# Key stacking moved ahead of the tree gathers in a perceiver kernel on one NeuronCore

## The chip, the cores and the metric

The kernel runs on one core of one Trainium2 chip. The metric is device time in microseconds (us) of one execution; lower is better. Engines in the text: PE (TensorE), DVE (VectorE), ACT (ScalarE), POOL (GpSimd), SP (SyncE, which issues transfers), and the 16 DMA engines of the core. The three runs shown gave 647.74, 648.18 and 651.8 us.

## The reference, cut to what matters

A residual stream `x` of 128 tokens by 128 features goes through twelve blocks; `ctx` has 2048 rows. Three blocks matter here: a linear attention (L1 attn), a block of four hard-routed trees (L1 ffn), and the cross attention behind it (L2 xattn), whose keys and values depend on `ctx` alone.

```python
def _fff(x, nw, nb, w1, b1, w2, b2, act):
    node = jnp.zeros(x.shape[:2], dtype=jnp.int32)
    for _ in range(DEPTH):                     # DEPTH = 8
        logit = jnp.einsum('bsd,bsd->bs', x, nw[node]) + nb[node]
        node = 2 * node + 1 + (logit > 0).astype(jnp.int32)
    leaf = node - NN
    h = act(jnp.einsum('bsd,bsdl->bsl', x, w1[leaf]) + b1[leaf])
    return jnp.einsum('bsl,bsld->bsd', h, w2[leaf]) + b2[leaf]
...
q = _fff(xn, q_nw, ...); k = _fff(xn, k_nw, ...); v = _fff(xn, v_nw, ...)
att = jax.nn.softmax(jnp.einsum('bqd,bkd->bqk', q, k) / jnp.sqrt(D), axis=-1)
...                                            # the fourth tree, f, runs on the sum of this attention and xn
x = x + _L1_attn_ref(...)
x = x + _L1_ffn_ref(...)
x = x + _L2_xattn_ref(_layernorm(x), ctx_1024, W_q, W_k, W_v, W_o, b_o)
```

Each of the 128 tokens picks its own leaf of 256, so each tree needs 128 leaves of 16 x 128 weights and 16 biases (first layer, 1.06 MB) and 16 x 128 weights and 128 biases (second layer, 1.11 MB).

## The kernel before, in words

The blocks run one after another; each is a Python function that appends its instructions to the five engines' streams (`l1a` the linear attention, `l1f` the trees, `cross` the cross attention). Each engine runs its own stream in order. Semaphores order the engines: `T`, `V`, `A`, `G` count steps of PE, DVE, ACT and POOL, and each transfer has its own (`loaded`). There is no scheduler; the order is written out by hand.

In `l1f`, PE turns the normalised tokens and computes the logits of all nodes of the trees q, k and v. DVE then walks the trees (`walk_vector`, first q, then k and v together) and writes one leaf number per token. POOL gathers the leaves by these numbers (`tree_gather`: two indirect transfers per tree, first and second layer; their places are in `leaves`). For each tree, DVE takes 16 products with running sums for the 16 units (`tree_vector`), DVE and ACT scale the second layer's weights by the units, eight rows of them each (`tree_scalar`), and PE sums 17 blocks of 128 x 128, each of them two passes (`tree_tensor`). Ahead of these stand `WARM` = 30 small bf16 products whose results nobody reads. The fourth tree, f, depends on the attention over q, k and v, so its walk and its gather come last.

Into this are woven the keys and values of the next cross attention. PE projects the keys from `ctxT` (four products of 512 columns, `keys_tensor`), ACT rounds them to a high half in `probsT` (`keys_scalar`), DVE subtracts to get the low half in `keysT` (`keys_vector`). The values (16 products, `values_tensor`) use the same banks, so they wait for the low halves; ACT copies them out (`values_scalar`). The high and low halves are then stacked from SBUF to SBUF by 13 transfers on SP's queue (`stack_keys`): twelve of 32 partitions by 8 KB, and one of 9 x 64 pieces of 512 bytes. Their destination holds the third leaf (tree k) until PE has summed it, so SP waits for that:

```python
leaves = {n: region[:, o:o + LEAF] for n, o in (("q", 0), ("v", LEAF), ("k", 2 * REG), ("f", 0))}
...
sp.wait_ge(T.sem, T.at(("o", "k")))
stack_keys(sp, "l2x", wide_high)
sp.wait_ge(T.sem, T.at(("o", "f")))
load("w_l2f", region[:, 0:REG], dram["w_l2f"])
```

Of the kernel before, what the change touches and what calls it, by code (L numbers as in the profile page):

```python
# [106 lines left out]
def build(nc, dram, out, scratch):  # L107
    ctx = ExitStack()
    with ctx:
# [74 lines left out]

        leaves = {n: region[:, o:o + LEAF] for n, o in (("q", 0), ("v", LEAF), ("k", 2 * REG), ("f", 0))}
        w_b_at = 2 * REG - width(W_B) - width(W_C)
# [102 lines left out]
        def _(sp):  # L289
# [19 lines left out]
            load("w_c", region[:, w_b_at + width(W_B):2 * REG], dram["w_c"])  # L309
            sp.wait_ge(T.sem, T.at(("o", "k")))  # L310
            stack_keys(sp, "l2x", wide_high)
# [34 lines left out]
        def turn_plan(tag):  # L346
            T.plan(tag + ".turned")
            V.plan(tag + ".T")
# [1007 lines left out]
        def l1a():  # L1356
# [8 lines left out]
            turn_plan("l1a.o")  # L1365
            T.plan("l1a.y")
            V.plan("l1a.x")

            @on("pe")
            def _(pe):  # L1370
# [13 lines left out]
                pe.wait_ge(V.sem, V.at("l1a.o.T"))  # L1384
                mm(ps[:, 0, 0:P], tG[:, :], at["w_l1a_p"]).then_inc(T.sem, T.now("l1a.y"))

            @on("dve")
            def _(dve):
# [14 lines left out]
                turn_vector(dve, "l1a.o", tG, 7)  # L1403
                end_vector(dve, tag, ps[:, 0, 0:P], xb[:, :], "l1a.y")

            @on("pool")
# [19 lines left out]
        def tree_gather(pool, n):  # L1426
            i = TREES.index(n)
            for layer, dst in ((1, leaves[n][:, 0:LEAF1]), (2, leaves[n][:, LEAF1:LEAF])):
                nc.gpsimd.indirect_dma_start(dst, None, dram[f"tree{layer}_{n}"], bass.IndirectOffsetOnAxis(
                    leaf_no[:, i:i + 1], 0)).then_inc(loads[f"leaf{layer}_{n}"], 16)  # L1430
# [5 lines left out]
        def second(n, c):  # L1436

            return leaves[n][:, LEAF1 + 4 * c * P:LEAF1 + 4 * (c + 1) * P]

        def tree_tensor(pe, n, turned):  # L1440
            o = ps[:, 4 + TREES.index(n), 0:P]

            loaded(pe, "leaf1_" + n)
            for _ in range(WARM):
                mm(ps[:, 0, 0:P], identb[:, :], identb[:, :])
            for c in range(4):
                made = A if c >= 2 else V
                pe.wait_ge(made.sem, made.at(("p", n, c)))
                for j in range(5 if c == 3 else 4):

                    w = second(n, c)[:, j * P:(j + 1) * P] if j < 4 else leaves[n][:, LEAF - P:LEAF]
                    if turned:
                        m = mm(o, w, ident, c == j == 0, j == 4)
                    else:
                        m = mm(o, ident, w, c == j == 0, j == 4)
            m.then_inc(T.sem, T.now(("o", n)))

        def tree_vector(dve, n, x, func=False):
            loaded(dve, "leaf1_" + n)
            h = units(n)  # L1460
            w1 = leaves[n]
            for j in range(LW):
# [64 lines left out]
        def l1f():  # L1527
# [6 lines left out]
            V.plan("l1f.xh")  # L1534
            turn_plan("l1f.xh")
            T.plan("l1f.nodes")
            T.plan(*(("l2x", "kp", b) for b in range(NB)))
            A.plan(*(("l2x", "k", b) for b in range(NB)))
            values_plan("l2x")
            V.plan("l1f.pathq", "l1f.paths", *(("l2x", "low", b) for b in range(NB)))  # L1540
            for n in "qkv":
# [9 lines left out]
            turn_plan("l1f.y")  # L1551
            T.plan("l1f.nodef")
            V.plan("l1f.pathf")
            tree_plan("f", True)
            V.plan("l1f.x")
# [3 lines left out]
            def _(pe):  # L1559
# [7 lines left out]

                loaded(pe, "w_b")
                for b in range(NB):
                    keys_tensor(pe, "l2x", at["w_b.l2x_k"], b, 3 + b)  # L1570
                values_tensor(pe, "l2x", at["w_b.l2x_v"], (7, 3, 4, 5), (None, 0, 1, 2))
                pe.wait_ge(A.sem, A.at(("l2x", "v", 3)))
                tree_tensor(pe, "q", True)
# [8 lines left out]
                pe.wait_ge(V.sem, V.at("l1f.y.T"))  # L1582
                mm(logits(0), xnT[:, :], nodew[:, 3 * NODES:4 * NODES]).then_inc(T.sem, T.now("l1f.nodef"))
                tree_tensor(pe, "f", False)

            @on("dve")
            def _(dve):
# [12 lines left out]
                                        ALU.mult).then_inc(V.sem, V.now("l1f.xh"))  # L1600
                turn_vector(dve, "l1f.xh", xnT)
                loaded(dve, "node")
                dve.wait_ge(T.sem, T.at("l1f.nodes"))
                walk_vector(dve, 0, 1, "l1f.pathq")
                dve.wait_ge(V.sem, V.at("l1f.pathq"))
                walk_vector(dve, 1, 2, "l1f.paths", 1)
                for b in range(NB):
                    keys_vector(dve, "l2x", None, b, 3 + b, wide_high)
                for n in "qkv":
# [23 lines left out]
            def _(act):  # L1633
                for b in range(NB):
                    keys_scalar(act, "l2x", None, b, 3 + b, wide_high)
                values_scalar(act, "l2x", (7, 3, 4, 5))
                for n in "qkv":
                    tree_scalar(act, n)
                act.wait_ge(V.sem, V.at("l1f.m"))
                nc.scalar.activation(tF[:, :], ps[:, 0, 0:P], ACT.Exp, bias=s[:, 1:2], scale=float(1.0 / np.sqrt(P)),  # L1640
                                     accum_out=s[:, 2:3]).then_inc(A.sem, A.now("l1f.p"))
                tree_scalar(act, "f", ACT.Gelu)

            @on("pool")
            def _(pool):
# [11 lines left out]
                pool.wait_ge(T.sem, T.at(("o", "q")))  # L1657
                tree_gather(pool, "f")


# [877 lines left out]
```

## Time and profile before

| what | us |
|---|---|
| runs | 647.74, 648.18, 651.8 (median 648.18) |
| the profiled execution's own time | 649.05 |
| its span in the trace | 647.2 |
| PE busy | 481.8 (74%) |
| DVE busy | 359.8 (56%) |
| ACT busy | 223.2 (34%) |
| POOL busy | 64.6 (10%) |
| DMA queue q1 (SP's transfers) | 33.71 MB, 15.8% of 16 engines' span |
| DMA queue q0 (POOL's gathers) | 8.68 MB, 3.8% |
| mean granted PE clock | 0.839 of full speed |

The busy time says which engine works most, but in a program of dependent blocks the time is set by the chain of waits: the list of instructions, in order of time, each of which released the next. Where one engine is on the chain alone, only that engine's work counts. PE's granted clock has two levels, 0.50 (1.2 GHz) and 1.00 (2.4 GHz). A row of the timeline gives start, duration, engine, source line, operation, what is written from what, and how often; a bracket at its end gives the idle time before it and what ended it.

### The profile page before, as it was taken

To read this page: it belongs to the slowest core of one execution; us is meant where nothing else is said; L and a number is where in the kernel's file an instruction comes from. 1 tells how busy PE (TensorE), PEld (TensorE's weight loads), DVE (VectorE), ACT (ScalarE), POOL (GpSimd) and SP (SyncE) were. 2 spreads that over 40 slices of the span, in tenths; PEclk is the share of its full clock that TensorE was granted. 3 is DMA by queue.
4 is the path that set the end of the run, shared out by engine and by line. 5 is a ranking of instruction groups with operands and counts; after the bars stand their busy time and mean duration, and the time that the engine had idled before them with its cause. 6 is when DMAs were issued, how large, how long until landed. Compare 5 with 4: busy or idle time off the path is not lost.

```text
span 647.2 us, 7837 instructions
## 1 busy us (share of the span) xinstructions
PE 481.8 (74%) x3019; PEld 351.1 (54%) x3019; DVE 359.8 (56%) x795; ACT 223.2 (34%) x439; POOL 64.6 (10%) x105
## 2 busy tenths in 40 slices
PE   3677638999656816799977565778999999866596
PEld 1545524443336805354434344657888888755496
DVE  7356448773349524777526555336666666634433
ACT  0212420778103301155632123316555555501021
POOL 5201002000013010200005104120000000000000
PEclk9787965999757956589988886968999999977679
DMA  7508200000418693600020000000000000045000
GB/s 299 251 3 177 85 1 0 1 1 2 194 53 333 169 180 135 260 1 1 2 90 8 0 1 0 2 1 1 1 1 1 1 1 2 1 162 228 0 1 6
DMA packets 8000, 42.89 MB, mean 66 GB/s; under 512 B 1050, under 2 KB 4122, under 8 KB 4762
## 3 DMA queue, kind: packets, MB, share of 16 engines
q1 hardware_dynamic: 6811, 33.71, 15.8%
q0 software_dynamic: 1152, 8.68, 3.8%
q8 instruction: 24, 0.39, 0.2%
q14 instruction: 13, 0.11, 0.1%
HBM read 35.69 MB, written 0.08 MB: 55 GB/s over the span
## 4 chain that ended last, share of the span: by engine, by line
PE 58%; DVE 28%; ACT 7%; issue 4%; DMA 2%; POOL 2%; POOLq 0%; DVEq 0%; ACTq 0%
PE banks L257 54%; PE banks L260 4%; DVE small L2044 3%; ACT probs L2119 3%; DVE peaks L1282 3%; DVE weights_lo L2054 2%; DMA region<-in_tree_f,leaf_no 2%; DVE xn L338 1%; POOL mv L344 1%; DVE sbq L1511 1%; ACT weights_hi L2132 1%; DVE tB L1786 1%; DVE xnT L357 1%; DVE tA L792 1%; DVE st L334 1%
## 5 line engine op out<-in xcount | busy, mean ns | idle before, releaser
L1282 DVE TENSOR_REDUCE peaks<-banks 128x1 f32<-128x1024 f32 x64 | 76.8, 1221 | 17.2 <-PE banks L257 17.0
L260 PE MATMUL banks<-p_first,probs 128*128 128x128 f32 x320 | 48.6, 288 | 16.6 <-DVE weights_lo L2054 4.4
L2044 DVE TENSOR_REDUCE small<-banks 128x1 f32<-128x1024 f32 x32 | 38.9, 1217 | 29.3 <-PE banks L257 29.3
L2132 ACT CAST weights_hi<-banks 128x512 fp32r<-128x512 f32 x64 | 35.9, 588 | 54.0 <-PE banks L260 54.0
L260 PEld LDWEIGHTS banks<-p_first,probs 128*128 128x128 f32 x320 | 38.3, 147 | 29.3 <-ACT probs L584 4.9
L1341 ACT ACTIVATE probs<-banks,seen 128x512 f32<-128x512 f32 x64 | 40.3, 685 | 27.2 <-PE banks L257 27.2
L2054 DVE TENSOR_TENSOR weights_lo<-banks,weights_hi 128x512 fp32r<-128x512 f32 x64 | 41.6, 682 | 13.0 <-ACT weights_hi L2132 13.0
L1341 ACT ACTIVATE probs<-banks 128x512 f32<-128x512 f32 x64 | 34.8, 595 | 32.9 <-PE banks L257 32.6
L344 POOL TENSOR_TENSOR mv<-mv,half 128x1 f32<-128x1 f32 x15 | 8.3, 553 | 344.8 <-DVE mv L336 344.8
L257 PE MATMUL banks<-probs,values 128*32 128x256 f32 x512 | 41.7, 395 | 0.4 <-DVE keysT L1303 0.4
L2119 ACT ACTIVATE probs<-banks,nmax 128x1024 f32<-128x1024 f32 x32 | 35.4, 1112 | 11.0 <-DVE nmax L2048 10.9
L257 PE MATMUL banks<-weights_hi,rows_hi 128*128 128x256 f32 x128 | 38.3, 299 | 0.0
L257 PE MATMUL banks<-xnT,region 128*128 128x128 f32 (+1 forms) x226 | 36.2, 322 | 1.9 <-DVE xnT L357 1.9
L257 PE MATMUL banks<-weights_lo,rows_hi 128*128 128x256 f32 x128 | 36.9, 288 | 0.0
L257 PE MATMUL banks<-weights_hi,rows_lo 128*128 128x256 f32 x128 | 36.7, 287 | 0.0
L257 PE MATMUL banks<-ctx_hi,query_r 128*128 128x512 f32 x64 | 28.7, 449 | 9.0 <-ACT probs L2119 6.5
L257 PEld LDWEIGHTS banks<-xnT,region 128*128 128x128 f32 (+1 forms) x226 | 33.4, 232 | 3.1 <-DVE xnT L357 3.1
L257 PE MATMUL banks<-keys_l1x,query_r 105*128 105x512 f32 x64 | 26.1, 503 | 4.3 <-DVE query_r L1164 3.2
L257 PE MATMUL banks<-keys_l2x,query_r 105*128 105x512 f32 x64 | 26.3, 507 | 3.3 <-DVE query_r L1164 2.2
L260 PE MATMUL banks<-p_first,xn 128*128 128x128 f32 x10 | 4.2, 418 | 32.6 <-DVE xn L338 32.6
L257 PE MATMUL banks<-region,probs 128*128 128x128 f32 x168 | 23.7, 286 | 4.1 <-ACT probs L670 2.1
L257 PE MATMUL banks<-ctx_hi,query_lo 128*128 128x512 f32 x64 | 26.7, 417 | 0.0
(422 smaller groups left out, 922.4 us busy)
## 6 DMA issues: line engine op xcount, KB each, us to landing
region<-in_w_l2f SPq DMA_DIRECT2D x1, 4096.0 KB, 13.0
region<-in_w_l3f SPq DMA_DIRECT2D x1, 4096.0 KB, 12.1
region<-in_w_b SPq DMA_DIRECT2D x1, 3076.0 KB, 10.3
values<-in_ctx SPq DMA_DIRECT2D x2, 1024.0 KB, 7.7
region<-in_w_l0f SPq DMA_DIRECT2D x1, 2048.0 KB, 20.4
keys_l1x<-shared SPq DMA_DIRECT2D x8, 256.0 KB, 3.9
keys_l2x<-probsT SPq DMA_DIRECT2D x8, 256.0 KB
region<-in_w_l3d SPq DMA_DIRECT2D x1, 2048.0 KB, 17.1
```

Of the source, the lines that this page charges most:

```text
L257: return nc.tensor.matmul(o, lhsT, rhs, start=start, stop=stop)
L260: return nc.tensor.transpose(o, i, ident[0:n, 0:n])
L334: vl(dve, nc.vector.bn_stats(st[:, :], src))
L338: nc.vector.tensor_scalar(xn[:, :], src, mv[:, 0:1], mv[:, 3:4], ALU.subtract, ALU.mult).then_inc(V.sem, V.now(tag + ".xn"))
L344: nc.gpsimd.tensor_tensor(mv[:, 3:4], mv[:, 2:3], half[:, 0:1], ALU.pow).then_inc(G.sem, G.now(tag + ".rstd"))
L357: nc.vector.tensor_copy(dst[0:n, :], ps[0:n, bank, 0:P]).then_inc(V.sem, V.now(tag + ".T"))
L1282: nc.vector.tensor_reduce(peaks[:, h // 4 % 2, i:i + 1], ps[:, 2 * a:2 * a + 2, :], AX.XY, ALU.max, negate=True).then_inc(VM.sem, VM.now(( ...
L1341: nc.scalar.activation(probs[:, u % 8 // 4, u % 4 * BANK:(u % 4 + 1) * BANK], ps[:, 4 + u % 3, :], ACT.Exp, scale=seen[:, 0:1] if masked e ...
L2044: return nc.vector.tensor_reduce(small[:, half:half + 1], ps[:, 2 * half:2 * half + 2, :], AX.XY, ALU.max)
L2054: nc.vector.tensor_tensor(sides(g, c, weights_lo), ps[:, 4 + c % 2, :].rearrange("p (a b) -> p a b", a=4), sides(g, c, weights_hi).bitcast ...
L2119: nc.scalar.activation(probs[:, g % 2, o:o + 2 * BANK], ps[:, 2 * half:2 * half + 2, :].rearrange("p a b -> p (a b)"), ACT.Exp, bias=nmax[ ...
L2132: nc.scalar.copy(sides(g, c, weights_hi), ps[:, 4 + c % 2, :].rearrange("p (a b) -> p a b", a=4)).then_inc(A.sem, A.now((tag, "e", g, c)))
```

## The change

The key projection of the next stage, its ACT halves and its place in the plans move from `l1f` to the end of `l1a`; DVE's low halves move ahead of the first walk. The value projection and its ACT copies move behind the logits of the fourth tree. The third leaf (k) no longer lies where the keys are stacked: its first layer goes to `probs`, its second to `values_t`. So SP's wait for that tree is gone. POOL writes the ones beside the values again, which the leaf has overwritten. The 30 idle products stay for q, become 44 for f, and go for k and v.

```diff
-        leaves = {n: region[:, o:o + LEAF] for n, o in (("q", 0), ("v", LEAF), ("k", 2 * REG), ("f", 0))}
+        spare = probs[:, :, :].rearrange("p a b -> p (a b)")
+        leaves = {n: (region[:, o:o + LEAF1], region[:, o + LEAF1:o + LEAF]) for n, o in (("q", 0), ("v", LEAF), ("f", 0))}
+        leaves["k"] = (spare[:, 0:LEAF1], values_t[:, 0:LEAF - LEAF1])
...
-            sp.wait_ge(T.sem, T.at(("o", "k")))
             stack_keys(sp, "l2x", wide_high)
...
                 mm(ps[:, 0, 0:P], tG[:, :], at["w_l1a_p"]).then_inc(T.sem, T.now("l1a.y"))
+                loaded(pe, "w_b")
+                for b in range(NB):
+                    keys_tensor(pe, "l2x", at["w_b.l2x_k"], b, 3 + b)
...
+            @on("act")
+            def _(act):
+                for b in range(NB):
+                    keys_scalar(act, "l2x", None, b, 3 + b, wide_high)
...
-            for _ in range(WARM):
+            for _ in range({"q": WARM, "f": 44}.get(n, 0)):
                 mm(ps[:, 0, 0:P], identb[:, :], identb[:, :])
...
-                loaded(pe, "w_b")
-                for b in range(NB):
-                    keys_tensor(pe, "l2x", at["w_b.l2x_k"], b, 3 + b)
-                values_tensor(pe, "l2x", at["w_b.l2x_v"], (7, 3, 4, 5), (None, 0, 1, 2))
-                pe.wait_ge(A.sem, A.at(("l2x", "v", 3)))
                 tree_tensor(pe, "q", True)
...
                 mm(logits(0), xnT[:, :], nodew[:, 3 * NODES:4 * NODES]).then_inc(T.sem, T.now("l1f.nodef"))
+                values_tensor(pe, "l2x", at["w_b.l2x_v"], (2, 3, 4, 5), (None,) * 4)
                 tree_tensor(pe, "f", False)
...
                 turn_vector(dve, "l1f.xh", xnT)
+                for b in range(NB):
+                    keys_vector(dve, "l2x", None, b, 3 + b, wide_high)
                 loaded(dve, "node")
...
                 walk_vector(dve, 1, 2, "l1f.paths", 1)
-                for b in range(NB):
-                    keys_vector(dve, "l2x", None, b, 3 + b, wide_high)
...
-                for b in range(NB):
-                    keys_scalar(act, "l2x", None, b, 3 + b, wide_high)
-                values_scalar(act, "l2x", (7, 3, 4, 5))
                 for n in "qkv":
                     tree_scalar(act, n)
...
+                values_scalar(act, "l2x", (2, 3, 4, 5))
                 tree_scalar(act, "f", ACT.Gelu)
...
                 tree_gather(pool, "f")
+                pool.wait_ge(T.sem, T.at(("o", "k")))
+                nc.gpsimd.memset(values_t[:, 0:KT_N * VW].rearrange("p (u w) -> p u w", w=PW)[:, :, 16:18],
+                                 1.0).then_inc(G.sem, G.now("l2x.ones"))
```

On PE, from the end of the linear attention (`p_w_a,tG` is its output projection) to the first product of the next cross attention, the kernel before has these rows; `ctxT,region` are keys, `region,ctxT` values, `identb` the idle products, and `shared,xnT` node logits:

```order
156 L257 MATMUL banks<-p_w_a,tG 128x128
157 L260 MATMUL banks<-p_first,tA 128x128
158 L257 MATMUL banks<-shared,xnT 128x255 x3
159 L257 MATMUL banks<-ctxT,region 128x512 x4
160 L257 MATMUL banks<-region,ctxT 128x128 x16
161 L257 MATMUL banks<-identb 128x128 x30
162 L257 MATMUL banks<-p_first,region 128x128 x17
163 L257 MATMUL banks<-identb 128x128 x30
...
171 L257 MATMUL banks<-shared,xnT 128x255
172 L257 MATMUL banks<-identb 128x128 x30
173 L257 MATMUL banks<-region,p_first 128x128 x17
```

The changed kernel has there:

```order
156 L259 MATMUL banks<-p_w_a,tG 128x128
157 L259 MATMUL banks<-ctxT,region 128x512 x4
158 L262 MATMUL banks<-p_first,tA 128x128
159 L259 MATMUL banks<-shared,xnT 128x255 x3
160 L259 MATMUL banks<-identb 128x128 x30
161 L259 MATMUL banks<-p_first,region 128x128 x17
162 L259 MATMUL banks<-p_first,values 128x128 x17
163 L259 MATMUL banks<-region,p_first 128x128 x17
...
168 L259 MATMUL banks<-shared,xnT 128x255
169 L259 MATMUL banks<-region,ctxT 128x128 x16
170 L259 MATMUL banks<-identb 128x128 x44
171 L259 MATMUL banks<-region,p_first 128x128 x17
```

The keys have moved ahead of the tokens' transpose, the values behind the fourth tree's logits, and the idle products of k and v are gone.

On SP, ahead of the stack of keys, the kernel before has:

```order
27 L283 DMA region<-in_w_b 128x6152 [waits vector_steps]
28 L283 DMA region<-in_w_c 128x1592
29 L283 DMA keys_l2x<-probsT 32x2048 [waits vector_steps,tensor_steps]
30 L283 DMA keys_l2x<-probsT 32x2048
31 L283 DMA keys_l2x<-keysT 32x2048
```

The changed kernel has:

```order
27 L285 DMA region<-in_w_b 128x6152 [waits vector_steps]
28 L285 DMA region<-in_w_c 128x1592
29 L285 DMA keys_l2x<-probsT 32x2048 [waits vector_steps]
30 L285 DMA keys_l2x<-probsT 32x2048
31 L285 DMA keys_l2x<-keysT 32x2048
```

The order is the same, but the stack now waits only for DVE's last low half, no longer for PE's third tree.

## Rows read from the trace of the kernel before

**Rows 1.** Chain of waits in the tree stage: start us, us, what.
```profile
180.99 0.81 PE banks L257 x2
...
186.07 0.36 DVE tA L1599
...
206.38 16.76 PE banks L257 x192
223.16 0.29 DVE tC L1612
...
233.81 10.86 DMA region<-in_tree_f,leaf_no
```

**Rows 2.** Timeline of PE: start us, us, engine, line, operation, passes [idle before].
```profile
187.39 2.92 PE L257 MATMUL banks<-shared,xnT 128*128 128x255 f32 x6 [0.38 <-DVE xnT L357]
190.10 4.80 PE L257 MATMUL banks<-ctxT,region 128*128 128x512 f32 x8
...
200.20 5.49 PE L257 MATMUL banks<-region,ctxT 128*128 128x128 f32 x24 [4.41 <-DVE keysT L1097]
...
206.38 1.85 PE L257 MATMUL banks<-identb 128*128 128x128 bf16 x30 [0.69 <-ACT values L1120]
...
219.11 4.01 PE L257 MATMUL banks<-region,p_first 128*128 128x128 f32 x34
...
244.71 3.38 PE L257 MATMUL banks<-identb 128*128 128x128 bf16 x30 [14.77 <-DMA region<-in_tree_f,leaf_no]
...
249.41 6.21 PE L257 MATMUL banks<-region,p_first 128*128 128x128 f32 x34 [1.32 <-DVE region L1477]
```

**Rows 3.** Timeline of DVE: walk q, low halves, start of trees q and v, products of v.
```profile
190.42 0.42 DVE L1500 TENSOR_TENSOR probs<-banks,shared 128x255 f32<-128x255 f32 x1 [3.08 <-PE banks L257]
...
199.47 2.48 DVE L1097 TENSOR_TENSOR keysT<-banks,probsT 128x512 f32<-128x512 f32 x4
...
201.86 0.28 DVE L1464 CUSTOM_DVE_ANT_0 region<-tA,region 128x128 f32<-128x128 f32 x1
...
212.34 0.29 DVE L1464 CUSTOM_DVE_ANT_0 region<-tA,region 128x128 f32<-128x128 f32 x1
...
216.27 1.29 DVE L1477 TENSOR_TENSOR region<-region,small 128x512 f32<-128x512 f32 x2
```

**Rows 4.** Windows: stretch, us, busy of each engine, granted PE clock, DMA share, GB/s.
```profile
192.00:194.00 2.00, 2.00 (x6) 0.84 (x5) 1.78 (x8) 1.17 (x2) 0.00 (x0) 0.87 0.00 0
...
196.00:198.00 2.00, 0.00 (x0) 0.00 (x0) 1.83 (x11) 0.42 (x1) 0.67 (x1) 1.00 0.84 190
198.00:200.00 2.00, 0.00 (x0) 0.00 (x0) 1.93 (x8) 0.00 (x0) 0.17 (x1) 0.84 1.00 404
...
197.00:213.00 16.00, 12.11 (x108) 11.81 (x109) 15.62 (x94) 6.12 (x18) 3.77 (x4) 0.79 0.97 394
219.00:233.00 14.00, 7.44 (x47) 5.56 (x44) 5.29 (x22) 1.74 (x3) 0.00 (x0) 0.77 0.97 203
235.00:241.00 6.00, 0.00 (x0) 0.00 (x0) 0.00 (x0) 0.00 (x0) 0.94 (x1) 0.50 0.92 114
```

**Rows 5.** Timeline of the issuing queues: SP's w_b, POOL's first v gather, SP's stack.
```profile
169.18 0.33 SPq L283 DMA_DIRECT2D region<-in_w_b  x1
...
202.31 0.94 POOL L1429 DMA_INDIRECT region<-in_tree_v,leaf_no  x1 [0.30 <-issue]
...
217.63 1.15 SPq L283 DMA_DIRECT2D keys_l2x<-probsT  x2
```

**Rows 6.** DMA issues: transfer, queue, how many, KB, median us from issue to landing.
```profile
region<-in_w_b SPq DMA_DIRECT2D x1, 3076.0 KB, 10.3
...
region<-in_tree_q,leaf_no POOLq DMA_INDIRECT x2, 6.4
...
region<-in_tree_v,leaf_no POOLq DMA_INDIRECT x2, 10.7
```

More of the change, by code:

```diff
@@ L1366, in l1a @@
             T.plan("l1a.y")
+            T.plan(*(("l2x", "kp", b) for b in range(NB)))
+            A.plan(*(("l2x", "k", b) for b in range(NB)))
             V.plan("l1a.x")
@@ L1427, in tree_gather @@
             i = TREES.index(n)
-            for layer, dst in ((1, leaves[n][:, 0:LEAF1]), (2, leaves[n][:, LEAF1:LEAF])):
+            for layer, dst in zip((1, 2), leaves[n]):
                 nc.gpsimd.indirect_dma_start(dst, None, dram[f"tree{layer}_{n}"], bass.IndirectOffsetOnAxis(
@@ L1436, in second @@
         def second(n, c):
-            return leaves[n][:, LEAF1 + 4 * c * P:LEAF1 + 4 * (c + 1) * P]
+            return leaves[n][1][:, 4 * c * P:4 * (c + 1) * P]
         def tree_tensor(pe, n, turned):
@@ L1449, in tree_tensor @@
                 for j in range(5 if c == 3 else 4):
-                    w = second(n, c)[:, j * P:(j + 1) * P] if j < 4 else leaves[n][:, LEAF - P:LEAF]
+                    w = second(n, c)[:, j * P:(j + 1) * P] if j < 4 else leaves[n][1][:, LW * P:]
                     if turned:
@@ L1460, in tree_vector @@
             h = units(n)
-            w1 = leaves[n]
+            w1 = leaves[n][0]
             for j in range(LW):
@@ L1535, in l1f @@
             turn_plan("l1f.xh")
+            V.plan(*(("l2x", "low", b) for b in range(NB)))
             T.plan("l1f.nodes")
[L1537 to L1540, printed above, removed]
+            V.plan("l1f.pathq", "l1f.paths")
             for n in "qkv":
@@ L1552, in l1f @@
             T.plan("l1f.nodef")
+            values_plan("l2x")
             V.plan("l1f.pathf")
+            G.plan("l2x.ones")
             tree_plan("f", True)
```

## The prediction

> **What bounds the kernel now.** I read the chain of waits first, since this is one core and one long dependent program: in the tree stage it names what each microsecond goes to. The stretch that the change touches runs from the end of the linear attention (180.99 us) to the first statistics of the next cross attention (about 255.6). The reader is to see three things in it [rows 1]. PE alone carries 206.38 to 223.16: three blocks of idle matmuls to keep the clock up and three sets of 17 transposes. Then follows a serial piece to 233.81 that the change leaves alone. Then 10.86 us are a pure wait for the gather of the fourth leaf. The timeline of PE says why the first block starts as late as 206.38: values of the next stage (24 passes, 5.49 us) stand ahead of it, and wait themselves for DVE's low halves of the keys, which end behind the walks [rows 2, 3]. It also shows the fourth tree's transposes at 6.21 us against 4.01 us for those of the third [rows 2].
>
> The DMA windows come next. While the six gathers of q, k and v run, all 16 engines are busy (share 0.97) at 394 GB/s; while the keys are stacked, they are just as busy (0.97) at 203 GB/s; and while the last, finely cut piece of the stack runs beside the fourth gather, 114 GB/s move in all [rows 4]. Before the change these two crowds are kept apart: gathers from about 197 to 213, stack from 217.63 [rows 4, 5]. DVE starts the third tree at 212.34, and the two v leaves take 10.7 us from issue at 202.31 (and 1.25 later) [rows 3, 5, 6]: that averages 213.65, and at 394 GB/s one leaf half of 1.09 MB takes 2.7, so the first half lands at about 212.3. DVE is therefore already fed by the DMA queue just in time.
>
> **The change, part by part.** All times are those of the profiled execution, span 647.2 us; its own time is 649.05, the median of the runs 648.18, so I add the difference to the median.
>
> *Key projection into the linear attention.* The weights pack w_b was issued at 169.18 and took 10.3, so it is there at 179.5, before PE finishes the linear attention at 181.80 [rows 1, 5, 6]. The eight passes took 4.80 us while the clock rose half way; at 1.2 GHz throughout, scaled from the node logits (2.92 us for six passes of 255 columns), they would take 7.8 [rows 2]. I take 5.9, because before, the clock rose on the way as well (mean 0.87 in the window of 192, after unbroken PE work from 187.39) [rows 2, 4]: 187.7 instead of 186.43 for the transpose that follows. ACT's copies lie beside it. The transpose and DVE's copy then end at 188.4, and four low halves (2.48 us, row of 199.47) come before the walk: DVE starts it at 190.9 instead of 190.42, +0.45. The node logits are hidden under the low halves. The same 2.48 us are gone behind the walks, but that frees DVE only to wait for leaf q.
>
> *The stack moves past the gathers.* SP no longer waits for the third leaf's place, so it issues 13 transfers at 190.9 rather than at 217.63. Twelve of them move 3.15 MB, 15.5 us at 203 GB/s [rows 4]. Bytes flow about 1.2 us after the issue, at 192.1; the gathers' bytes, 0.45 later than before, at 197.45. So 5.35 us of the stack are over and 10.1 us remain, beside 16.5 us of gathers. No row has two streams of long rows at once, so I bound it. If the engines only take turns, the gathers lose all 10.1 us; if the stack's half rate leaves 394 - 203 = 191 GB/s usable, they lose 5.2. The last piece runs about 6 us in which a gather gets 114 - 49 = 65 GB/s (0.29 MB are its own), a loss of 5.0. With the 0.45 the first half of v lands at 227.9 or at 222.95 instead of 212.3; between ends that no row decides I take the middle, 225.4.
>
> The Trainium skill ("DMA: Bandwidth & Descriptors", section "Queues, rings and completion order") says each engine goes round robin over its queues packet by packet; by that the gathers get no precedence, and the sum is the turn-taking one. The same skill ("SBUF — State Buffer", section "Door 1: The DMA port swizzle") says 32 partitions reach only half of the SBUF ports, which would explain 203 beside 394 and speaks for the other bound. Neither is used in the sum.
>
> *Trees.* From the start of a tree DVE needs 216.27 - 212.34 = 3.93 us to its units and 0.65 to the first product, PE then 4.0 for 17 transposes [rows 2, 3]. The dropped idle matmuls of k and v would give back 2 x 1.85 us [rows 2], were PE still the bound; it no longer is. With v at 225.4, k comes some 6 us earlier, PE starts k's transposes cold at about 224 and needs 6.2 (as the fourth tree's), ends at 230.2, and v's then 234.2. Before it was 223.12 [rows 2]: **+11.1 us** (+8.4 and +13.4 at the ends).
>
> *Fourth leaf.* Its gather finds an empty queue. The q leaf did: 6.4 us from issue to landing [rows 6]; now 10.86 [rows 1]. **-4.5 us.**
>
> *Values and 44 idle matmuls before the fourth tree.* Sixteen products (32 passes, at 5.49/24 = 0.23 us each at most 7.3 us) run during the gather wait, which is 6.4 us behind the walk's 3.5: hidden by 2.6 us. Then 44 idle matmuls at 3.38/30 each take 4.96 us, DVE needs 4.7 for the first product, so they delay PE by 0.3, but the transposes then run at 4.01 instead of 6.21 us: **-1.9 us**. PE stood still from 196 on and the clock fell in the window of 198 (mean 0.84) [rows 4]; after the values PE stands still as long, so the 44 must do the warming alone; if they don't, the term is +0.3. ACT's four value copies and its table load end before the leaf. POOL's memset stands behind the last gather and nobody waits for it. The new home of the third leaf changes no shape and no count.
>
> Sum: +11.1 - 4.5 - 1.9 = **+4.7 us**, so 648.2 + 4.7 = **652.9 us**. The likeliest case alone spans +2.0 (8.4 - 6.4) to +7.0 (13.4 - 6.4): 650.2 to 655.2.
>
> **The rivals.** (1) *No collision.* The engines serve both streams without loss, or stack rows slip into gaps. Then the DMA order is as before: v at 212.75, units at 216.7, PE ends at 221.4, -1.8 against 223.12; with -6.4 this is -8.2, 640.0 us. For it: the stack never gets beyond half of the rate that the engines can do. Against: share 0.97 in both streams. 12%. (2) *The gathers come first*, the stack gives way and its fine piece falls behind v: say the gathers lose a quarter of the turn-taking 15.6, about 4: -1.8 + 4 - 6.4 = -4.2, 644.0. Against it: beside the stack's last piece the fourth gather got only 65 GB/s. 13%. (3) *Slower by more than the mean of the noise:* a long stack row holds an engine while a gather's row waits, so gathers crawl as they do at 235 to 241 for the whole time, and PE, idle between trees now that the idle matmuls are gone, transposes v cold as well: 13.4 + 2.2 - 6.4 = +9.2, 657.4; it decides from the point where PE stands still before v as long as from 196 to 199. If the fourth gather's 10.86 were not the stack's doing, +4.5 comes on top of the forecast instead, 657.4 as well. 20%. The forecast keeps 55%.
>
> **How the numbers follow.** A measurement here can tell about 1% (6.5 us) from no change. Faster than 641.7 needs rival 1: 0.12. Slower than 654.7 takes rival 3 and the upper tenth of the forecast's 55%: 0.26. The rest, 0.62, is within 1%. The range 642.5 to 658.0 leaves out rival 1 and little above rival 3.
>
> **What would show it.** In the profile after: stack issues at 191 (else the argument's start is wrong); both queues busy in 197 to 217 with a rate between 200 and 394 GB/s; DVE idle before trees k and v, released by DMA (if PE releases it, I am wrong about the new bound); the third tree's last transpose at 231 to 237; the fourth gather at 6.4 us and its transposes at 4.0. If the gathers keep 394 GB/s beside the stack, the forecast falls and rival 1 stands.

## The result, and the profile after

The changed kernel took **662.67 us** (median of four runs, 662.38 to 665.15) beside 649.99 for the kernel before: ratio 1.0203, 95% interval 1.0172 to 1.0234. I had forecast 652.9 with a range up to 658.0. So it is slower by 12.7 us where I had said 4.7, and outside the range. A second measurement of the same kernel in a later batch, told further down, gave 656.92 beside 649.40, ratio 1.0128 (1.0089 to 1.0166). The two intervals do not meet; both say slower, by 0.9% at the least. Slow executions, more than 1.5% above the fastest of their kernel, are left out of the ratios and medians below: two of the four of hold_ones (687.83 and 2303.34 us) and three of the six of hold_ones3 (648.11, which is only just over that line, 806.31 and 1457.38 us).

The profiled execution has a span of 660.3 us, 13.1 more than before. The chain of waits through the tree stage of the changed kernel (start us, us, what) answers to [rows 1]:

```profile
205.24 29.91 DMA region<-in_tree_v,leaf_no
...
236.08 5.67 PE banks L259 x34
241.78 0.29 DVE tC L1619
...
251.97 6.61 DMA region<-in_tree_f,leaf_no
258.63 8.88 PE banks L259 x78
267.53 0.30 DVE xs L377
```

Where PE carried 16.76 us without a gap, a transfer now does: 29.91 us from the issue of the second v gather to its data. Behind it the fourth leaf's wait has shrunk from 10.86 to 6.61 us. The timeline of DVE in the same kernel (last bracket: idle before, and what ended it) answers to [rows 3]; it starts with the first walk:

```profile
192.11 0.41 DVE L1511 TENSOR_TENSOR probs<-banks,shared 128x255 f32<-128x255 f32 x1
...
207.07 0.29 DVE L1475 CUSTOM_DVE_ANT_0 region<-tA,region 128x128 f32<-128x128 f32 x1 [5.83 <-DMA region<-in_tree_q,leaf_no]
215.07 1.29 DVE L1488 TENSOR_TENSOR region<-region,small 128x512 f32<-128x512 f32 x2 [4.09 <-DMA region<-in_tree_q,leaf_no]
222.05 0.29 DVE L1475 CUSTOM_DVE_ANT_0 probs<-tA,probs 128x128 f32<-128x128 f32 x1 [5.69 <-DMA probs<-in_tree_k,leaf_no]
228.91 0.29 DVE L1475 CUSTOM_DVE_ANT_0 region<-tA,region 128x128 f32<-128x128 f32 x1 [1.63 <-DMA region<-in_tree_v,leaf_no]
235.24 1.29 DVE L1488 TENSOR_TENSOR region<-region,small 128x512 f32<-128x512 f32 x2 [2.42 <-DMA region<-in_tree_v,leaf_no]
```

DVE waits for each leaf, and for q and v twice: for the first half and again, before the products, for the second. Q's second wait costs nothing by itself, since the k leaf lands later still. The timeline of PE (start, us, passes, idle before), for [rows 2]:

```profile
183.09 6.28 PE L259 MATMUL banks<-ctxT,region 128*128 128x512 f32 x8
...
226.83 6.90 PE L259 MATMUL banks<-p_first,values 128*128 128x128 f32 x34 [5.36 <-DVE values L1488]
236.08 5.66 PE L259 MATMUL banks<-region,p_first 128*128 128x128 f32 x34 [2.36 <-DVE region L1488]
...
247.90 4.70 PE L259 MATMUL banks<-region,ctxT 128*128 128x128 f32 x32
258.63 4.88 PE L259 MATMUL banks<-identb 128*128 128x128 bf16 x44 [6.03 <-DMA region<-in_tree_f,leaf_no]
263.33 4.16 PE L259 MATMUL banks<-region,p_first 128*128 128x128 f32 x34
```

The transposes of q, k and v, each behind a wait, run slower than 4.0 us (5.66, 6.90 and 5.66); those of the fourth tree, which took 6.21 before, take 4.16. The windows (stretch, us, busy of PE, its weight loads, DVE, ACT and POOL, granted clock, DMA share, GB/s) show the stack alone, stack beside gathers, gathers beside what is left of the stack, and the end, for [rows 4]:

```profile
193.00:199.00 6.00, 0.00 (x0) 0.00 (x0) 5.38 (x26) 0.00 (x0) 2.15 (x2) 0.69 0.97 197
204.00:219.00 15.00, 6.57 (x45) 6.30 (x46) 5.13 (x36) 2.44 (x8) 1.88 (x2) 0.50 1.02 242
222.00:229.00 7.00, 2.17 (x10) 2.20 (x11) 5.22 (x37) 2.45 (x8) 0.00 (x0) 0.79 1.02 357
229.00:235.00 6.00, 4.72 (x26) 4.53 (x25) 3.75 (x34) 0.00 (x0) 0.00 (x0) 0.68 0.54 76
```

Together the two streams move 242 GB/s with the DMA engines busy throughout (share 1.02). The last window is the second half of the v leaf beside the finely cut piece of ones: 76 GB/s. SP's timeline has the stack from 192.22, its last issue at 203.74:

```profile
192.22 1.15 SPq L285 DMA_DIRECT2D keys_l2x<-probsT  x2
...
203.74 0.94 SPq L285 DMA_DIRECT2D keys_l2x<-one  x1
```

I measure from now on between three landmarks that every kernel here has in its timelines: **y**, the start of the linear attention's output projection on PE (before 180.99), **tC**, DVE's first copy behind the third tree's transposes (223.16), and **xs**, the first write behind the fourth tree (255.66). From y to tC the kernel before takes 42.17 us and the changed one 59.28: +17.1. From tC to xs 32.50 and 25.75: -6.75. Before y it is late by 1.5 and behind xs by 1.2; both lie in code that the change does not touch, and no run explains them. Over the 14 profiles y lies anywhere from 180.2 to 184.4 us.

### The profile page after: what moved, and what is told of

Its sections match the earlier page's. It is cut to its first block, busy times and chain, and to the rows that moved or that the text cites. A ratio compares the mean times of both kernels' runs of the same rounds, so it can differ in the third digit from the quotient of the medians.

```text
span 660.3 us, 7746 instructions
## 1 busy us (share of the span) xinstructions
PE 487.4 (74%) x2973; PEld 356.7 (54%) x2973; DVE 360.0 (55%) x795; ACT 223.4 (34%) x439; POOL 64.9 (10%) x106
## 4 chain that ended last, share of the span: by engine, by line
PE 56%; DVE 26%; ACT 6%; DMA 6%; issue 4%; POOL 2%; POOLq 0%; DVEq 0%; ACTq 0%
PE banks L259 52%; DMA region<-in_tree_v,leaf_no 5%; PE banks L262 4%; DVE small L2052 3%; ACT probs L2127 3%; DVE peaks L1283 3%; DVE weights_lo L2062 2%; DVE xn L339 1%; POOL mv L345 1%; DMA region<-in_tree_f,leaf_no 1%; ACT weights_hi L2140 1%; DVE tB L1794 1%; DVE sbq L1522 1%; DVE tA L793 1%; DVE xnT L358 1%
## 5 line engine op out<-in xcount | busy, mean ns | idle before, releaser
L2127 ACT ACTIVATE probs<-banks,nmax 128x1024 f32<-128x1024 f32 x32 | 35.4, 1112 | 11.1 <-DVE nmax L2056 10.9
L259 PE MATMUL banks<-ctx_lo,query_r 128*128 128x512 f32 x64 | 26.4, 412 | 0.0
```

What stands on the lines that cost most here:

```text
L259: return nc.tensor.matmul(o, lhsT, rhs, start=start, stop=stop)
L2127: nc.scalar.activation(probs[:, g % 2, o:o + 2 * BANK], ps[:, 2 * half:2 * half + 2, :].rearrange("p a b -> p (a b)"), ACT.Exp, bias=nmax[ ...
```

## The experiments

Each batch has its own runs of the kernel before, on the same chip as the rest of the batch. The chips on record are number 2 (gate_back, hold, ones_early, hold_ones, and in a later batch after_warm, hold_ones3 and hold_ones_warm2), 12 (hold_ones2, hold_ones_warm, split6, before_late_ones) and 8 (after_again); that of the first result is not on record. The last three columns are of the one profiled execution, in us.

| kernel | median us | ratio to before, 95% | y to tC | tC to xs | xs to end |
|---|---|---|---|---|---|
| before | 648.18 to 650.28 | 1 | 42.17 | 32.50 | 391.5 |
| after | 662.67 | 1.0203 (1.0172-1.0234) | 59.28 | 25.75 | 392.8 |
| after_again | 656.92 | 1.0128 (1.0089-1.0166) | 56.15 | 25.89 | 391.0 |
| after_warm | 657.62 | 1.0142 (1.0087-1.0196) | 55.17 | 25.58 | 392.4 |
| ones_early | 654.56 | 1.0108 (1.0050-1.0165) | 53.00 | 25.53 | 392.0 |
| split6 | 646.48 | 0.9966 (0.9948-0.9983) | 43.02 | 25.48 | 392.3 |
| gate_back | 647.42 | 0.9991 (0.9970-1.0011) | 40.14 | 30.38 | 392.4 |
| hold | 647.51 | 0.9988 (0.9961-1.0015) | 40.37 | 30.66 | 390.6 |
| before_late_ones | 646.23 | 0.9955 (0.9936-0.9975) | 42.18 | 25.60 | 395.2 |
| hold_ones | - | - | 39.99 | 25.87 | 394.0 |
| hold_ones2 | 645.44 | 0.9948 (0.9922-0.9974) | 40.21 | 25.15 | 397.5 |
| hold_ones3 | 639.01 | 0.9822 (0.9765-0.9878) | 40.77 | 25.57 | 393.0 |
| hold_ones_warm | 641.80 | 0.9906 (0.9879-0.9933) | 39.04 | 25.90 | 390.7 |
| hold_ones_warm2 | 642.79 | 0.9876 (0.9836-0.9916) | 40.07 | 25.71 | 391.6 |

**Is it the early stack at all?** The theory says that the whole loss is the stack running beside the gathers. The rival is that something else in the change costs it: the keys ahead of the walk, the missing idle products, the third leaf's new home. *gate_back* gives the changed kernel its old wait and nothing else; *hold* gives SP a lighter one, for the v leaf's landing.

```diff
+            sp.wait_ge(T.sem, T.at(("o", "k")))
             stack_keys(sp, "l2x", wide_high)
```

> The changed kernel with one part undone: SP waits again for the third tree's sum before it stacks the keys; all else stays. Theory (the stack's transfers beside the gathers are the loss): the gathers run alone at about 394 GB/s, v's second half lands some 20 us earlier than in the changed kernel, the last v transpose ends 1.8 us sooner than in the kernel before (relative to the end of the linear attention), and the fourth tree gains its 2 us; the fourth gather still meets the fine piece, 8 to 11 us. Time 642 to 646 against 650.0. Rival (the dropped idle matmuls and the moved low halves are the loss, through PE's clock): nothing but the gathers changes, PE's transposes stay at 5.7 to 6.9 us a tree, and the time stays above 654.

```diff
+            loaded(sp, "leaf2_v")
             stack_keys(sp, "l2x", wide_high)
```

> The changed kernel, but SP waits for the second half of the v leaf to land before it stacks the keys. Collision theory: no two streams at once until the fourth gather; v's end as in gate_back; the stack starts 1 to 3 us later than there, so the fourth gather meets more of the fine piece: 9 to 11 us instead of 6.6. Time 643 to 647. Clock rival: above 654.

Both fell back to the time of the kernel before (ratios 0.9991 and 0.9988); gate_back's median lies 1.4 us above the 642 to 646 that I expected, hold's half a microsecond above 647. The timeline of DVE in *hold* shows the q, k and v leaves nearly as they were:

```profile
201.66 0.29 DVE L1476 CUSTOM_DVE_ANT_0 region<-tA,region 128x128 f32<-128x128 f32 x1 [1.25 <-DMA region<-in_tree_q,leaf_no]
...
208.06 0.29 DVE L1476 CUSTOM_DVE_ANT_0 probs<-tA,probs 128x128 f32<-128x128 f32 x1 [1.17 <-DMA probs<-in_tree_k,leaf_no]
...
213.46 0.29 DVE L1476 CUSTOM_DVE_ANT_0 region<-tA,region 128x128 f32<-128x128 f32 x1 [0.18 <-DMA region<-in_tree_v,leaf_no]
...
244.13 0.29 DVE L1476 CUSTOM_DVE_ANT_0 region<-tB,region 128x128 f32<-128x128 f32 x1 [11.31 <-DMA region<-in_tree_f,leaf_no]
```

So moving the stack alone accounts for the loss in this stretch: y to tC is 40.4 with it held and 59.3 or 56.2 without. The rest of the change is worth -1.8 us there (40.37 against 42.17), the figure that my rival without a collision had. And the fourth gather waits 11.31 us again when the stack is late, which keeps the time from falling. One thing stays open: from y to xs the two profiles are 4.2 and 3.6 us shorter than that of the kernel before (70.52 and 71.03 against 74.67), a gain that the ratios of the run times do not show.

**Which part of the stack?** *ones_early* takes the finely cut piece (288 KB of ones) out of the stack and sends it at 90 us, where nothing waits for it; the twelve other transfers stay early.

```diff
             load("node", nbias, dram["nbias"].partition_broadcast(P))
+            sp.wait_ge(V.sem, V.at("l0f.x"))
+            stack_ones("l2x")
... (stack_ones is the piece's transfer, taken out of stack_keys)
```

> The changed kernel, with the finely cut piece of the stack (576 pieces of 512 B of ones) issued long before, during the cross attention ahead; the other twelve transfers still meet the gathers. If the fine piece makes the tail (v's second half lands 6.3 us behind its first in the changed kernel, 2.7 in the one before), that distance falls to about 3 us and the time to 657 or 658. If the twelve large transfers make the tail, it stays at 6 and the time at 662.

It took 654.56 us, below what I expected; but its interval (1.0050 to 1.0165) overlaps that of after_again, so the gain over the changed kernel is read from the profiles, not from the run times. Its DVE rows:

```profile
220.98 0.29 DVE L1479 CUSTOM_DVE_ANT_0 probs<-tA,probs 128x128 f32<-128x128 f32 x1 [5.34 <-DMA probs<-in_tree_k,leaf_no]
...
226.43 0.29 DVE L1479 CUSTOM_DVE_ANT_0 region<-tA,region 128x128 f32<-128x128 f32 x1 [0.22 <-DMA region<-in_tree_v,leaf_no]
```

The wait for v's second half is gone (no DMA wait between 226.43 and the fourth leaf), so that wait, 2.42 us in the first profile of the changed kernel and 2.17 in the second, was the fine piece's. What the twelve cost is left: k starts 38.70 us behind y (220.98 - 182.28), in *hold* 26.13, so 12.6 us more. Both are single profiles; over all seven with the stack held, k starts 24.6 to 26.1 us behind y, which puts the cost at 12.6 to 14.1. The piece by itself, in a stretch that it shares with nothing, moved 44 GB/s over six microseconds (window of ones_early):

```profile
91.00:97.00 6.00, 2.52 (x9) 1.97 (x9) 1.57 (x7) 1.73 (x5) 0.56 (x1) 0.50 0.38 44
```

**Does the loss follow the bytes that overlap?** *split6* lets six of the twelve go at once and holds the other six for the v leaf; the fine piece is early as above.

```diff
                     load("keys_" + tag, keys_r[tag][32 * part:32 * part + 32, t, :].bitcast(F32), src)
+                    if tag == "l2x" and 3 * t + part + 1 == 6:
+                        loaded(sp, "leaf2_v")
```

> The fine piece early; the first six of the twelve transfers at once, the other six held until v's second half has landed. Six take 7.8 us at 203 GB/s, of which about 5 run before the gathers' first bytes. If the loss is the overlap alone, the gathers lose 3 to 5 us, most of it at q, and v's first half lands 3 to 5 us later than in hold_ones: 645 to 648. If any stacking beside gathers upsets them for good, v lands as late as in ones_early: 654.

It took 646.48, as expected. The six leave k starting 29.03 us behind y (row below, y at 183.61), 2.9 more than in hold (up to 4.4 beside the other profiles with the stack held), and tC 2.65 later. Q, the first leaf to land, starts 3.9 us later than in hold (23.60 against 19.73), so one of its microseconds is made up by k:

```profile
207.21 0.29 DVE L1481 CUSTOM_DVE_ANT_0 region<-tA,region 128x128 f32<-128x128 f32 x1 [5.96 <-DMA region<-in_tree_q,leaf_no]
212.64 0.29 DVE L1481 CUSTOM_DVE_ANT_0 probs<-tA,probs 128x128 f32<-128x128 f32 x1 [0.20 <-DMA probs<-in_tree_k,leaf_no]
```

By turn-taking, six transfers (7.75 us at 203 GB/s) of which 5.35 are over when the gathers begin should cost 2.4 us; by the bound with usable spare rate, 1.2. With twelve the two bounds are 10.1 and 5.2, and 12.6 was measured. Both points lie above the turn-taking end, never near the other. What the engines lose above turn-taking (at k 0.5 us or more with six, 1.5 at q, and 2.5 or more with twelve) I can only describe: in the mixed window they moved 242 GB/s. Why it is more than turn-taking stays open.

**What holds up the fourth leaf?** *before_late_ones* is the kernel before with one edit: the fine piece waits until the fourth leaf has landed.

```diff
             stack_keys(sp, "l2x", wide_high)
+            loaded(sp, "leaf2_f")
+            stack_ones("l2x")
... (stack_ones as in ones_early)
```

> The kernel before, with the fine piece of the stack held until the fourth leaf's second half has landed (it then has 8 us until the cross attention asks for the keys). If the fine piece alone holds up the fourth gather, that gather falls from 10.9 to about 6.5 us and the time by 4.3 us to 644.9 against 649.2; if the twelve large transfers ahead of it do, it stays near 10.

It took 646.23 (expected 644.9). In its DVE timeline the fourth leaf comes 6.45 us after DVE began to wait, and the piece has become a wait of its own ahead of the next cross attention:

```profile
239.98 0.29 DVE L1468 CUSTOM_DVE_ANT_0 region<-tB,region 128x128 f32<-128x128 f32 x1 [6.45 <-DMA region<-in_tree_f,leaf_no]
...
251.67 0.48 DVE L1265 MEMSET keysT<- 32x512 f32 x1 [2.57 <-DMA keys_l2x<-one]
```

So the 288 KB of the fine piece, and not the 3.15 MB of the twelve, were what the fourth gather waited for in the kernel before: tC to xs fell from 32.50 to 25.60. Whether it is the short rows is not shown: the piece also lies on nine partitions only, and no run separates the two. Of the 6.9 us, some 2 are not the gather's: the fourth tree's transposes took 4.06 us here, behind the shorter wait, and 6.21 before, with the same 30 idle products. Its PE timeline has the row, and the windows behind it show how the fourth gather, issued at 233.81, starts with nothing beside it (last figure: GB/s):

```profile
244.71 4.06 PE L257 MATMUL banks<-region,p_first 128*128 128x128 f32 x34 [1.32 <-DVE region L1481]
```

```profile
234.81:235.81 1.00, 0.00 (x0) 0.00 (x0) 0.00 (x0) 0.00 (x0) 0.76 (x1) 0.50 0.87 116
235.81:236.81 1.00, 0.00 (x0) 0.00 (x0) 0.00 (x0) 0.00 (x0) 0.18 (x1) 0.50 0.73 149
236.81:237.81 1.00, 0.00 (x0) 0.00 (x0) 0.00 (x0) 0.00 (x0) 0.00 (x0) 0.50 0.77 322
```

It gains less at the end of the program because xs to end grew by 3.7, of which the row above shows 2.57.

**Both repairs together.** *hold_ones* holds the twelve and sends the fine piece early, by the edits of hold and ones_early; *hold_ones2* and *hold_ones3* are the same kernel in two later batches. Of the first try, expected at 641.5, only the profile is used (span 641.9); the two executions left gave 643.67 and 641.32.

> Both: the fine piece early, the twelve transfers held until v's second half has landed. Collision theory: gathers alone, stack alone from 215 to 232, and the fourth gather alone (6.4 us): 641.5, the sum of all gains (-1.8 -0.4 -4.3 -2.0 on 650.0). Clock rival: above 652.

> The same kernel as hold_ones again (fine piece early, twelve transfers held until v's second half has landed), because its timing was disturbed while its profile was not. From that profile (span 641.9 beside 644.0 and 643.6 for gate_back and hold): collision theory 642 to 644, some 1% under the kernel before. A rival by which the early fine piece costs the cross attention ahead something would give 647.

> Both edits together once more (the twelve stack transfers held until the v rows have landed, the fine piece of ones sent early), with no idle matmuls added. It is here to stand beside the next kernel on one chip. Expected 644 to 646, ratio 0.993 to 0.996.

The chain of waits of hold_ones2 has the two gathers at

```profile
201.37 10.52 DMA region<-in_tree_v,leaf_no
...
230.74 6.32 DMA region<-in_tree_f,leaf_no
```

Ratios 0.9948 (expected 642 to 644, measured 645.44) and 0.9822 (expected 644 to 646, measured 638.08 to 641.71): faster than the kernel before both times, by an amount that differs between the two batches and that I missed both times, once on each side. The 0.9822 rests on three timings only, so how much faster is not settled. In the profiles the gain at xs is the same each time: y to xs takes 65.9, 65.4 and 66.3 us in the three profiles against 74.67, so 8.3 to 9.3 us less. How much of it reaches the end varies with the rest of the program.

**Cold transposes and the missing idle products.** The v transposes of the changed kernel took 5.66 us. *hold_ones_warm* and *after_warm* put 30 idle products back before the k and v transposes.

```diff
-            for _ in range({"q": WARM, "f": 44}.get(n, 0)):
+            for _ in range({"q": WARM, "f": 44}.get(n, WARM)):
```

> hold_ones with the 30 idle matmuls ahead of the k and v trees put back. If dropping them cost clock, PE's 17 transposes of k and v fall below the 4.03 us of hold_ones and the time falls; my reading is that the clock is already up there (4.03 us each), that 30 of them take 1.8 us while PE waits for the first product anyway, and that nothing changes: within 0.3% of hold_ones.

> As the kernel before this one, plus 30 idle matmuls for k and 30 for v in the tree stage. In the first try its profile ran 7.5 us less than its neighbour's, yet the tree stage itself was no shorter (softmax behind the transposes at 219.3 against 220.8, the xs copy at 245.2 against 245.9); the rest lay beyond 300 us, in stages that neither edit touches. If the idle matmuls do nothing, the two medians agree within 0.2% here, near 645. If they help by the clock of the tree stage alone, 1 to 2 us: 643 to 644.5. If the 641.8 of the first try was theirs, it comes back: 641 to 642.5.

> The changed kernel with 30 idle matmuls while PE waits for the tree stage's k rows and 30 for the v rows (q has its own already, f its 44); nothing else differs. Theory (three terms: wait of the v rows' first half at the turn-taking bound, wait for their second half, and cold v transposes): the v transposes lie after the v rows' second half has landed, so their 5.66 us at half clock are on the path; warm they take the 4.0 to 4.1 us that they take in the kernels with the stack held back, and the kernel gains 1.6 us: 660.5 to 661.5 beside 662.4 to 662.9, ratio to the kernel before about 1.018. Rival: the cold clock costs nothing on its own, since the v transposes are paced by the products that DVE makes for them; then their row stays over 5 us with the clock at 1.00 and the time does not move. Second rival: the idle matmuls also lift the clock of the softmax and value work behind the transposes, and the gain is 3 us or more.

The PE timeline of after_warm, around v:

```profile
228.79 1.84 PE L259 MATMUL banks<-identb 128*128 128x128 bf16 x30
231.91 4.06 PE L259 MATMUL banks<-region,p_first 128*128 128x128 f32 x34 [1.28 <-DVE region L1488]
```

The transposes run warm, 4.06 us. But the median, 657.62, was 5 us below the changed kernel's first, and 3 below what I had expected; that is three times what 1.6 us of transposes can explain. Another 2.4 us lay in an earlier landing of the v leaf. To see whether that was spread, the unedited changed kernel ran once more:

> The changed kernel itself, unedited, a second time. With warm k and v transposes the profile gained 4.1 us from the start of the output projection to the end of the v transposes, of which 1.6 are the transposes and 2.4 the landing of the v rows' second half (50.3 us behind that start, against 52.7 in the first profile of the changed kernel). If those 2.4 us are the spread of the transfers from one execution to the next, this profile may put the second half anywhere from 50 to 53 us behind the start, and the v transposes are cold again at 5.6 to 5.7 us; median 660 to 663. If the landing has to do with the idle matmuls, it comes at 52.5 to 53 us again, and the median is 662 to 663.

656.92 us, and the v leaf's second half lands early too. Rows of DVE, then of PE, in its timelines:

```profile
226.62 0.29 DVE L1475 CUSTOM_DVE_ANT_0 region<-tA,region 128x128 f32<-128x128 f32 x1 [0.88 <-DMA region<-in_tree_v,leaf_no]
232.70 1.29 DVE L1488 TENSOR_TENSOR region<-region,small 128x512 f32<-128x512 f32 x2 [2.17 <-DMA region<-in_tree_v,leaf_no]
...
233.54 4.03 PE L259 MATMUL banks<-region,p_first 128*128 128x128 f32 x34 [1.72 <-DVE region L1488]
```

The v products start 51.24 us behind y (181.46) where the first profile had 52.74, and here v was transposed warm with no idle product before it. My expectation that it would be cold again was wrong, and the median lies 3 us below the 660 to 663 that went with it. So after_warm (ratio 1.0142) and the unedited kernel in its second batch (1.0128) cannot be told apart: the idle products before k and v are worth nothing that I could measure in the changed kernel. With the stack held the picture is no clearer: 641.8 and 642.8 with them, 645.4 and 639.0 without; y to tC 39.0 and 40.1 against 40.0, 40.2 and 40.8. On chip 12 the products seemed to gain 0.4% (0.9906 against 0.9948, where I had expected no change within 0.3%), on chip 2 to lose 0.5% (0.9876 against 0.9822): no gain is shown. The 642.79 of hold_ones_warm2 lies between the outcomes that I had listed and decides for none.

## Why the prediction was wrong, point by point

**The keys in the linear attention: right.** I took 5.9 us; they took 6.28 (5.65 in the second profile). The first walk starts 9.61 us behind y (192.11 - 182.50), before 9.43; I had 9.9. The stack is issued at 192.22, 9.7 behind y, as forecast.

**Trees, +11.1 us: wrong, and this is the step that failed.** It came out at +17.1, and at +14.0 in the second profile. What failed is the landing of the v leaf: I took the mean of two bounds for its first half, put the wait for its second half at nothing, and left the cold transposes to a rival. In the order of the sum:

- "Between ends that no row decides I take the middle." The middle put v's first half 44.4 us behind y, turn-taking 46.9. It was 46.4 (228.91 - 182.50) and 45.2 in the second: +2.0 and +0.75. That this is so little is luck, for its two parts were off in opposite directions. The middle allowed 7.65 us for the twelve transfers; ones_early shows 12.6, above even turn-taking's 10.1. For the fine piece I took 5.0 us; v's first half lands 44.15 us behind y without it (ones_early), so the piece cost 2.3 and 1.0 there (0.1 in after_warm).
- The 5.0 us came from the window of 235:241, whose low rate I charged to the piece. But the fourth gather starts slowly alone, too: in before_late_ones it moves 116 and 149 GB/s in the second and third microsecond behind its issue at 233.81, and 322 in the fourth. And beside gathers already under way the piece left far more than the 114 GB/s of that window: 357 GB/s from 222 to 229 in the changed kernel.
- The second half of v. I let it land 2.7 us behind the first, hidden under DVE's 3.93. DVE had to wait 2.42 (second profile 2.17) for it. I had put the fine piece's slow stretch ahead of v; it ran beside v's second half, at the end of both queues, and there nothing hides it. ones_early, without the piece, has no such wait. (Q's second half, too, landed 8.0 us behind its first, 215.07 - 207.07, and that also without the piece: 7.5 in ones_early.)
- Cold v transposes, which I had only in a rival: 5.66 us instead of 4.0 in the first profile (+1.7), none in the second (4.03).

2.0 + 2.4 + 1.7 = 6.1 against the 6.0 that the term was short; for the second, 0.75 + 2.2 = 2.95 against 2.9. Over the whole stretch that I priced, y to xs, the kernel grew by 10.4 us (7.4 in the second profile) against my 4.7; the other 2.7 us of the first profile lie outside it.

The rule of the Trainium skill that I weighed and left out of the sum, round robin over the queues ("DMA: Bandwidth & Descriptors", section "Queues, rings and completion order"), would have given the turn-taking end for the twelve, 10.1 us; the 12.6 of the traces are nearer to it than to the middle's 7.65, but above it. That 32 partitions reach half the ports ("SBUF — State Buffer", section "Door 1: The DMA port swizzle") may explain 203 beside 394 GB/s, but the half left over was not to be had by the gathers: 242 in the mixed window.

**Fourth leaf, -4.5: right.** 10.86 became 6.61, -4.25, 6.40 in the second. before_late_ones shows the reason given for it, the queue without the stack, and narrows it to the fine piece.

**Values and 44 idle products, -1.9: right in size, its cause in part open.** The 32 passes took 4.70 us, not the 7.3 that I scaled from a stretch at a granted clock of 0.50; they end at 252.6 and PE then stands idle for 6.0 us, so they are hidden. From the leaf to xs (267.53 - 258.58) it took 8.95 us, before 10.99 (255.66 - 244.67): -2.0. The transposes took 4.16. With gate_back and hold they took 4.06 behind waits of 11 to 12 us, where the kernel before, with 30 idle products, took 6.21; so there the 44 or the values ahead of them do the warming. In the changed kernel the wait is short, and before_late_ones has 4.06 behind such a wait with the old 30: that the 44 were needed here is not shown.

**The rivals.** No collision (640.0) and gathers first (644.0) are excluded by 242 GB/s and by the DVE waits. Rival 3 (657.4) came nearest, by turn-taking and cold v transposes, but not by its own mechanism: it let the gathers crawl as at 235 to 241, where they got 65 GB/s, and beside the stack they moved about 145 (the 2.17 MB of q's second and k's first half between 207.07 and 222.05). V was transposed cold in one of the two profiles. It lacked the wait for v's second half. I had given it 20% and kept 55% for a middle that no mechanism stood behind; that is why 662.67 lay outside the range. The spread between batches, 5.7 us for one and the same kernel, I had not allowed for at all: the second measurement, 656.92, would have been inside.

## What to carry to other kernels

Between two bounds that stand for two mechanisms, the middle stands for none: price each mechanism for itself, and where both streams show a share of 0.97 each, let the sum be turn-taking until a row shows otherwise; here it was 0.5 to 4 us more. Before a window's rate is charged to one of two streams, look at each alone: here some 3 of the 7 slow microseconds were the gather's own start. When a transfer moves ahead of others on the same engines, look at what comes last in both queues, since here the second half of the last leaf met the slowest piece. And a small, finely cut transfer can be what a large one waits for: here the version that beat both kernels sends 288 KB of ones over 100 us earlier and keeps the 3.15 MB where they were.

## What the runs showed of the hardware

- 288 KB in rows of 512 bytes moved at 44 GB/s on nine partitions with the DMA engines busy for a share of 0.38 (ones_early, 91 to 97 us), so something other than the engines' own time limited it; what, no run shows. Yet a gather that started beside it was held as well: the fourth leaf landed 10.86 to 11.74 us behind its issue in the three kernels that have the piece beside it (before, gate_back, hold), and 6.2 to 6.6 us behind it in all the others. A gather already under way was held less: 357 GB/s moved in all.
- A gather starts slowly with nothing beside it: 116, 149, 322 and 430 GB/s in the second to fifth microsecond behind its issue (before_late_ones, fourth leaf).
- Long SBUF to SBUF rows beside gathers from HBM gave 242 GB/s at share 1.02 in the changed kernel, where the two alone gave 203 and 394. The twelve transfers, with by estimate 10.1 us of their own work left when the gathers began, delayed these by 12.6 to 14.1 (ones_early beside the seven profiles with the stack held).
- The same program gives different ratios on different chips or at different times (1.0203 and 1.0128; 0.9948 and 0.9822), with intervals that do not meet. One part of it seems to be PE's clock in stages that no edit touches. Windows of hold_ones2, then of hold_ones_warm, over the same stretch:

```profile
360.00:420.00 60.00, 40.06 (x245) 32.90 (x246) 27.27 (x54) 15.43 (x47) 13.60 (x20) 0.76 0.00 1
```

```profile
360.00:420.00 60.00, 37.22 (x262) 30.86 (x263) 27.76 (x55) 17.78 (x50) 12.77 (x23) 0.86 0.00 1
```

The granted clock is 0.76 and 0.86, and xs to end 397.5 and 390.7. Over all of xs to end the same 1989 PE instructions are busy for 316.2 us at 0.84 in hold_ones2 and for 307.7 at 0.87 in hold_ones_warm, while DVE's stay at 218. That the clock makes the whole of these 6.8 us was not tested. Differences of half a percent between kernels in different batches say nothing here.
